# Graph attention: the decay and the division of a visit's sums moved from VectorE to GpSimd, between its gathers

## Chip, cores and metric

One Trainium2 chip, of which the kernel uses one core. The metric is the device time of one execution in microseconds (us), the median of several runs. The engines are TensorE (PE; its weight loads are PEld), VectorE (DVE), ScalarE (ACT), GpSimd (POOL) and SyncE (SP), which issues most transfers.

## What is computed

Four graph layers follow one another on 1250 nodes, 21250 edges and 1024 features, each with a residual sum and a layer norm behind it: a product with a sparse weight, graph attention, a graph convolution, and two neighbour-mean layers. The change lies in the attention:

```python
xl = (x @ Wl).reshape(n, H, D)
xr = (x @ Wr).reshape(n, H, D)
msg = xl[src] + xr[dst]
act = jnp.where(msg > 0, msg, NEG_SLOPE * msg)
e = jnp.einsum('ehd,hd->eh', act, att)
m = jax.ops.segment_max(e, dst, num_segments=n)
p = jnp.exp(e - m[dst])
denom = jax.ops.segment_sum(p, dst, num_segments=n)
alpha = p / (denom[dst] + 1e-16)
out = jax.ops.segment_sum(alpha[..., None] * xl[src], dst, num_segments=n)
```

with 4 heads of 64 columns.

## The kernel before

The attention is one loop over 23 visits (SUBS). A visit takes 55 nodes (SUB) and a window of 1024 edges, which are sorted by their target; the window has two halves (QUADS, index a), each of 4 tiles of 128 edges. A visit's work is spread over several visits' time, and each engine has its own program, written out by hand; semaphores alone tie them together. The main step i counts quarters of a visit, four to a visit.

- **GpSimd** gathers the rows xl[src]: for each half four indirect transfers of 128 rows (gather_half, L507, issued at L509). It has seven buffers (GOT), so the gather for a half waits until VectorE has weighed the half seven before (L1286), and with each new visit for that visit's source indices (L1282). In time, GpSimd gathers the second half of visit J+1 and the first half of visit J+2 while the other engines are at visit J.
- **SP** loads per visit the source indices (L1201), the targets spread over all partitions (L1206), the targets as columns (L1209) and the rows of xr (L1217). After the loads of visit j it stores the mixed rows of visit j-5 (STORE_LAG; store, L1245 to L1248, which waits for out_ready); then come a fetch of a weight tile for the later layers in some visits (L1223, visits 4, 4, 5, 5, 6, 9, 12, 15, 18, 21), in visit 17 loads for the next stage (load_ahead, L1236), and then the loads of visit j+1, the source indices first.
- **TensorE** forms the messages (L1308, L1313: it turns the gathered rows and adds the target's row), scores them (L1320), spreads scores (L1330), subtracts the new maximum (take_shift, L1336), turns the shifted score rows (turn, L1344) and sums the weighed rows per node (mix, L1353).
- **ScalarE** scales messages (L1430), marks nodes (L1419, L1425), takes the exponentials of the scores (L1450) and of the fall of the maximum (keep_sums, L1441): the factors by which older sums decay.
- **VectorE** bends messages (L1492), finds maxima (L1500), marks edges (L1524), clamps scores (L1530), weighs the gathered rows with the exponentials (weigh, L1537, two instructions a visit), splits a weight tile in some visits (low, L1568) and closes a visit with finish (L1543): the decay of the node's old sums (L1549), the addition of TensorE's new sums (L1552), a guard of the denominators (L1555), their reciprocal (L1557) and the division, a multiplication into the mixed rows (L1561). finish of visit j-3 is the last work of the main visit j; the clamp of the next visit stands right behind it.

The old sums are not zero before the first visit: they hold each node's own loop edge. They lie in one tile for all visits (summed), so no visit waits for another's sums.

Of the kernel before, what the change touches and what calls it, by code (L numbers as in the profile page):

```python
# [18 lines left out]
ALU = mybir.AluOpType  # L19
# [5 lines left out]
FEAT, HID, HEADS = 1024, 256, 4  # L25
HEAD_DIM = HID // HEADS
# [7 lines left out]
SUB = 55  # L34
SUBS = -(-NODES // SUB)
# [471 lines left out]
def gather_half(nc, got, src, a, xl_d, landed):  # L507
    for t in range(QUAD):
        nc.gpsimd.indirect_dma_start(got[:, t, :], None, xl_d,  # L509
                                     bass.IndirectOffsetOnAxis(src[:, a * QUAD + t:a * QUAD + t + 1], 0))\  # L510
            .then_inc(landed, 16)
# [593 lines left out]
def attention_stage(nc, g, src_d, dst_d, xl_d, xr_d, best, summed, x1_d, mixed_d, fetched, first_src, first_got,  # L1105
# [12 lines left out]
    with nc.Fori(0, rounds) as again, ExitStack() as ctx:  # L1118
        m = Memory(nc, ctx, "attention")

        def slots(name, shape, dtype=F32, n=2):
            return [m.sb(f"{name}{s}", shape, dtype) for s in range(n)]
# [17 lines left out]
        keep = slots("keep", [SUB, HEADS])  # L1140
        hot = slots("hot", [P, SUB_TILES + 1, SUB])
        weighted = slots("weighted", [P, SUB_TILES, HEADS, HEAD_DIM + 1])
        inverse = m.sb("inverse", [SUB, HEADS])
        mixed = slots("mixed", [SUB, HID])
        nothing = m.sb("nothing", [ROWS - SUB * SUBS, HEAD_DIM])
        message_ps = [m.ps(f"message_ps{s}", [P, HALF]) for s in range(2)]
# [16 lines left out]
        fall_ready, shift_ready, shifted, shifted_out, turned, clamp_ready, exp_ready, keep_ready, hot_ready = (  # L1163
            m.sem(n) for n in
            "fall_ready shift_ready shifted shifted_out turned clamp_ready exp_ready keep_ready hot_ready".split())
        weighed, mixed_in, out_ready = (m.sem(n) for n in "weighed mixed_in out_ready".split())
        best_found, lowered, summed_up, guarded, inverted = (
            m.sem(n) for n in "best_found lowered summed_up guarded inverted".split())
# [4 lines left out]
        mixed_stored = m.sems("mixed_stored")  # L1173
        block = m.block(gpsimd_works=True)

        def held(j, a):
            return got[(j * QUADS + a) % GOT]
# [7 lines left out]
        def half_of(u):  # L1185
            return u % QUADS, u // QUADS

        def pair_of(u):
            a, k = half_of(u)
            return 2 * (a * KH + k), 2 * (a * KH + k) + 2  # L1190

        @block.sync
        def _(sp):
# [83 lines left out]
        @block.gpsimd  # L1277
        def _(pool):
            for j in range(SUBS):
                s = j % 3  # L1280
                if j >= 1:
                    pool.wait_ge(src_ready[s], 16 * (j // 3 + (1 if s else 0)))  # L1282
                for a in range(QUADS):
                    n = j * QUADS + a
                    if n >= GOT:
                        pool.wait_ge(weighed, n - GOT + 1)  # L1286
                    if n >= 1:
                        gather_half(nc, held(j, a), src[s], a, xl_d, got_ready[n % GOT])
            pool.wait_ge(next_src, 16)
            pool.wait_ge(weighed, (SUBS * QUADS - 1) // GOT * GOT + 1)  # L1290
            gather_half(nc, first_got, first_src, 0, xl_d, next_got)
            pool.wait_ge(next_got, 16 * QUAD)

        @block.tensor
        def _(pe):
# [28 lines left out]
            def spread(j, u):  # L1324
                i = j * UNITS + u
                if u == 0:
                    pe.wait_ge(rows_ready, j + 1)
                elif i >= 2:
                    pe.wait_ge(maxed, i - 1)
                nc.tensor.matmul(spread_ps[u % 2][:, :], picked(g, *pair_of(u)), score_rows[:, :],  # L1330
                                 start=True, stop=True).then_inc(spread_out, 1)
# [81 lines left out]
        def _(act):  # L1413
# [23 lines left out]
            def keep_sums(j):  # L1437
                b = j % 2
                by_part = keep[b][:, :].rearrange("p (k t) -> p t k", t=2)
                for part in range(2):  # L1440
                    last = nc.scalar.activation(by_part[:, part, :], fall[b][part * PART:part * PART + SUB, :], ACT.Exp)  # L1441
                last.then_inc(keep_ready, 1)
# [19 lines left out]
            for i in range(LAST + 2 * UNITS):  # L1462
                j, q = i // UNITS, i % UNITS
                if q == 0 and 2 <= j <= SUBS + 1:
                    exponentials(j - 2)
                if i < LAST:
                    scale(i)
                if q == 0 and 2 <= j <= SUBS + 1:
                    keep_sums(j - 2)
                if q == 0 and j in SPLIT_VISITS:  # L1470
                    high(SPLIT_VISITS.index(j))
                if q == 1 and 1 <= j <= SUBS:
                    take_rows(j - 1)
                if q == (1 if j == 0 else 2) and j + 1 < SUBS:
                    mark_far(j + 1)
                if q == (2 if j == 0 else 3) and j + 1 < SUBS:
                    find_nodes(j + 1)
                if i == LAST + 2:
                    act.wait_ge(ahead_turned, 1)
                    nc.scalar.activation(ahead_hi[:, :], message_ps[0][:, 0:HID], ACT.Copy).then_inc(ahead_high, 1)  # L1480
                if q == 3 and 1 <= j <= SUBS:
                    take_shifted(j - 1)
# [3 lines left out]
        def _(dve):  # L1486
# [56 lines left out]
            def finish(j):  # L1543
                b = j % 2
                whole = summed[0:SUB, j]
                if j == SUBS - 1:
                    dve.wait_ge(keep_ready, j + 1)
                dve.wait_ge(mixed_in, j + 1)
                nc.vector.tensor_tensor(whole, whole, keep[b][:, :].unsqueeze(2)  # L1549
                                        .to_broadcast([SUB, HEADS, HEAD_DIM + 1]), ALU.mult).then_inc(lowered, 1)  # L1550
                dve.wait_ge(lowered, j + 1)
                nc.vector.tensor_tensor(whole, mix_ps[b][0:SUB, 0:HEADS * (HEAD_DIM + 1)]  # L1552
                                        .rearrange("p (h d) -> p h d", h=HEADS), whole, ALU.add).then_inc(summed_up, 1)
                dve.wait_ge(summed_up, j + 1)
                nc.vector.tensor_scalar(inverse[:, :], whole[:, :, HEAD_DIM], 1e-16, None, ALU.add).then_inc(guarded, 1)  # L1555
                dve.wait_ge(guarded, j + 1)
                nc.vector.reciprocal(inverse[:, :], inverse[:, :]).then_inc(inverted, 1)  # L1557
                dve.wait_ge(inverted, j + 1)
                if j >= 2:
                    dve.wait_ge(mixed_stored[b], 16 * (j // 2))  # L1560
                nc.vector.tensor_tensor(mixed[b][:, :].rearrange("p (h d) -> p h d", h=HEADS), whole[:, :, 0:HEAD_DIM],  # L1561
                                        inverse[:, :].unsqueeze(2).to_broadcast([SUB, HEADS, HEAD_DIM]), ALU.mult)\
                    .then_inc(out_ready, 1)

            def low(n):
                k, columns = n // 2, slice(n % 2 * HALF, (n % 2 + 1) * HALF)
# [32 lines left out]
            for i in range(LAST + 3 * UNITS):  # L1599
                j, q = i // UNITS, i % UNITS  # L1600
# [758 lines left out]
```

## Time and profile before

| | us |
|---|---|
| median of 3 runs | 1559.93 |
| lowest and highest run | 1555.97, 1564.11 |
| span of the profiled execution, first to last instruction | 1553.5 |
| busy in it: TensorE | 1433.6 |
| VectorE | 783.6 |
| ScalarE | 421.9 |
| GpSimd | 254.4 |

The profiled execution is known by its span; the runs' times lie 2.5 to 10.6 us above it. The attention runs from about 310 to 650 us of the span; ahead of it the graph is built and the first layer computed, behind it come the other layers, in which TensorE works almost without a break. A row of the timeline has the start, the duration, the engine, the line of the kernel, the operation, what it writes and reads, and in brackets how long the engine was idle before it and what ended that. "issue" means that the profile shows nothing for which it waited; SPq is SP's queue, where a row is the issue of a transfer.

### The profile page before, as it was taken

How to read it: one execution, taken by the hardware profiler on the slowest of the kernel's cores; microseconds unless marked ns; L12 is line 12 of the kernel's file. 1: busy time of each engine (PE TensorE's matmuls, PEld its weight loads, DVE VectorE, ACT ScalarE, POOL GpSimd, SP SyncE). 2: the span in 40 equal slices, each digit the busy share in tenths (PEclk: the TensorE clock that was granted, in tenths of full speed). 3: DMA queues.
4: the chain of work that ended last, by engine and by line, in shares of the span. 5: the costliest groups of instructions: out<-in, count | busy, mean ns of one | idle time of the engine just before them, and what ended most of it. 6: DMA issues, size and time to landing. Idle time of an engine off the chain costs nothing.

```text
span 1553.5 us, 17781 instructions
## 1 busy us (share of the span) xinstructions
PE 1433.6 (92%) x6845; PEld 1145.2 (74%) x6845; DVE 783.6 (50%) x1359; ACT 421.9 (27%) x716; POOL 254.4 (16%) x309
## 2 busy tenths in 40 slices
PE   3988999748999989899999999999999999999996
PEld 3876888625666656678888888888888888888884
DVE  6996776517888868754336632221033232411243
ACT  7853222235565545312111100110120001201000
POOL 3000000064666655110000010000000100000000
PEclk9997999969999999999999999999999999999998
DMA  1665344454555644152117552230056544400252
GB/s 46 192 181 189 106 126 116 93 157 150 163 155 153 179 146 130 55 185 85 61 42 240 180 189 85 103 145 1 0 190 219 187 124 147 143 1 0 91 194 95
DMA packets 101988, 195.95 MB, mean 126 GB/s; under 512 B 26856, under 2 KB 61465, under 8 KB 101905
## 3 DMA queue, kind: packets, MB, share of 16 engines
q1 hardware_dynamic: 77434, 121.01, 25.8%
q0 software_dynamic: 22800, 73.61, 13.9%
q8 instruction: 54, 0.88, 0.2%
q10 hardware_dynamic: 1670, 0.21, 0.1%
q14 instruction: 30, 0.24, 0.0%
HBM read 140.86 MB, written 53.92 MB: 125 GB/s over the span
## 4 chain that ended last, share of the span: by engine, by line
PE 56%; DVE 1%; DMA 0%; issue 0%; POOL 0%; DVEq 0%; ACT 0%
PE layers_y_ps L1927 35%; PE layers_y_ps L1948 17%; PE layers_turn_ps L1911 2%; PE layers_up_ps L1894 1%; PE layers_y_ps L1964 1%; DMA x_d<-fetched_x 0%; DVE layers_w_lo L2082 0%; DVE layers_y L2126 0%; PE layers_y_ps L1972 0%; DVE layers_y L597 0%; DVE layers_ln_stats L591 0%; PE layers_turn_ps L1882 0%; DVE layers_parts_lo L2099 0%; DVEq L592 0%; PE layers_y_ps L1882 0%
## 5 line engine op out<-in xcount | busy, mean ns | idle before, releaser
L1948 PE MATMUL layers_y_ps<-layers_parts_hi,layers_counts 128*128 128x512 f32 x464 | 143.6, 391 | 0.0
L1948 PE MATMUL layers_y_ps<-layers_parts_lo,layers_counts 128*128 128x512 f32 x464 | 143.3, 390 | 0.0
L1927 PE MATMUL layers_y_ps<-layers_w_hi,layers_parts_hi 128*128 128x512 f32 x400 | 126.0, 396 | 0.0
L1927 PE MATMUL layers_y_ps<-layers_w_lo,layers_parts_hi 128*128 128x512 f32 x400 | 123.6, 390 | 0.0
L1927 PE MATMUL layers_y_ps<-layers_w_hi,layers_parts_lo 128*128 128x512 f32 x400 | 123.5, 390 | 0.0
L509 POOL DMA_INDIRECT attention_got<-xl_d,attention_src x104 | 106.5, 1024 | 63.1 <-DVE attention_weighted L1537 31.3
L1948 PEld LDWEIGHTS layers_y_ps<-layers_parts_lo,layers_counts 128*128 128x128 f32 x464 | 87.1, 188 | 18.7
L1948 PEld LDWEIGHTS layers_y_ps<-layers_parts_hi,layers_counts 128*128 128x128 f32 x464 | 86.9, 188 | 18.9
L1353 PE MATMUL attention_mix_ps<-attention_weighted,attention_hot 128*110 128x260 f32 x368 | 95.7, 384 | 3.7 <-DVE attention_weighted L1537 3.7
L1320 PE MATMUL attention_row_ps<-attention_bent,edges_att_rows 128*128 128x512 f32 x184 | 97.1, 611 | 0.0
L2099 DVE SCALAR_TENSOR_TENSOR layers_parts_lo<-layers_y_ps,layers_parts_hi 128x1024 fp32r<-128x1024 f32 x16 | 19.6, 1225 | 147.5 <-ACT layers_parts_hi L2043 147.5
L2093 DVE TENSOR_TENSOR layers_parts_lo<-layers_turn_ps,layers_parts_hi 128x1024 fp32r<-128x1024 f32 x24 | 29.4, 1224 | 125.8 <-ACT layers_parts_hi L2037 125.8
L2037 ACT ACTIVATE layers_parts_hi<-layers_turn_ps 128x1024 fp32r<-128x1024 f32 x24 | 24.6, 1026 | 246.6 <-PE layers_turn_ps L1911 246.6
L1353 PEld LDWEIGHTS attention_mix_ps<-attention_weighted,attention_hot 128*110 128x110 f32 x368 | 61.9, 175 | 38.5 <-DVE attention_weighted L1537 14.9
L1927 PEld LDWEIGHTS layers_y_ps<-layers_w_lo,layers_parts_hi 128*128 128x128 f32 x400 | 75.1, 188 | 16.4
L1927 PEld LDWEIGHTS layers_y_ps<-layers_w_hi,layers_parts_lo 128*128 128x128 f32 x400 | 75.1, 188 | 16.1
L1927 PEld LDWEIGHTS layers_y_ps<-layers_w_hi,layers_parts_hi 128*128 128x128 f32 x400 | 73.3, 188 | 14.4
L1927 PE MATMUL layers_y_ps<-fetched_w_hi,layers_parts_hi 128*128 128x512 f32 x240 | 76.0, 398 | 0.0
L1927 PE MATMUL layers_y_ps<-fetched_w_lo,layers_parts_hi 128*128 128x512 f32 x240 | 75.5, 395 | 0.0
L1927 PE MATMUL layers_y_ps<-fetched_w_hi,layers_parts_lo 128*128 128x512 f32 x240 | 75.4, 395 | 0.0
L1492 DVE TENSOR_TENSOR attention_bent<-attention_message_ps,attention_scaled 128x512 f32<-128x512 f32 x92 | 61.8, 685 | 22.8 <-issue 11.8
L1430 ACT ACTIVATE attention_scaled<-attention_message_ps 128x512 f32<-128x512 f32 x92 | 54.4, 591 | 68.2 <-PE attention_message_ps L1313 45.3
(341 smaller groups left out, 2783.4 us busy)
## 6 DMA issues: line engine op xcount, KB each, us to landing
layers_counts<-counts_d SPq DMA_DIRECT2D x30, 640.0 KB, 4.0
layers_rest<-x_d SPq DMA_DIRECT2D x23, 512.0 KB, 4.1
self_d<-layers_y POOLq DMA_DIRECT2D x20, 512.0 KB, 6.0
x_d<-layers_y POOLq DMA_DIRECT2D x19, 512.0 KB, 2.9
fetched_x<-x_d SPq DMA_DIRECT2D x17, 512.0 KB, 3.7
fetched_raw<-in_L_gnn_W_self POOLq DMA_DIRECT2D x16, 512.0 KB, 5.9
fetched_raw<-in_L_gnn_W_neigh POOLq DMA_DIRECT2D x16, 512.0 KB, 9.0
heads_dst_wide<-in_dst_held SPq DMA_DIRECT2D x13, 512.0 KB, 4.0
```

The lines of the kernel that those rows point to most:

```text
L509: nc.gpsimd.indirect_dma_start(got[:, t, :], None, xl_d, bass.IndirectOffsetOnAxis(src[:, a * QUAD + t:a * QUAD + t + 1], 0))\
L1320: nc.tensor.matmul(row_ps[j % 2][:, :], g["att_rows"][:, k, (1 - a) * HEADS:(1 - a) * HEADS + P], bent[i % 3][:, :], start=(i % UNITS == 0 ...
L1353: last = nc.tensor.matmul(mix_ps[j % 2][0:2 * SUB, 0:HEADS * (HEAD_DIM + 1)], hot[j % 2][:, t:t + 2, :].rearrange("p t n -> p (t n)"), wei ...
L1430: nc.scalar.activation(scaled[i % 2][:, :], message_ps[i % 2][:, :], ACT.Copy, scale=SLOPE)\
L1492: nc.vector.tensor_tensor(bent[i % 3][:, :], message_ps[i % 2][:, :], scaled[i % 2][:, :], ALU.max)\
L1894: last = nc.tensor.matmul(up_ps[:, a:a + HALF], rows_in[t % 2][:, k, :], w[k][:, a:a + HALF], start=(k == 0 and p == 0), stop=(k == KH - 1 ...
L1911: last = nc.tensor.transpose(turn_ps[:, k * P:(k + 1) * P], rows_in[:, k * P:(k + 1) * P], g["ident"][:, :])
L1927: last = nc.tensor.matmul(y_ps[n % 2][:, a:a + HALF], rows_in[t][:, k * P:(k + 1) * P], w[k][:, a:a + HALF], start=(k == 0 and p == 0), st ...
L1948: last = nc.tensor.matmul(y_ps[n % 2][:, a:a + HALF], counts[c % 2][:, k, :], part[k][:, a:a + HALF], start=(k == 0 and part is hi), stop= ...
L2037: nc.scalar.activation(hi[t], turn_ps[:, :], ACT.Copy).then_inc(turned_high, 1)
L2093: nc.vector.tensor_tensor(lo[t], turn_ps[:, :], hi[t].bitcast(F32), ALU.subtract).then_inc(turned_low, 1)
L2099: nc.vector.scalar_tensor_tensor(out=lo[t], in0=y_ps[n % 2][:, :], scalar=scale, in1=hi[t].bitcast(F32), op0=ALU.mult, op1=ALU.subtract).t ...
```

## The change

The decay (now lower) and the division (now divide) of every visit but the last go to GpSimd. In GpSimd's visit j the decay of visit j-4 stands between the two blocks of gathers, and the division of visit j-5 behind the second block; the rest follows the last gathers. The reciprocals get a second buffer. ScalarE's keep factors wait until those of two visits before have been used, since they have two buffers. For the last visit VectorE does both itself.

```diff
-        inverse = m.sb("inverse", [SUB, HEADS])
+        inverse = slots("inverse", [SUB, HEADS])
...
+        def lower(engine, queue, j):
+            whole = summed[0:SUB, j]
+            queue.wait_ge(keep_ready, j + 1)
+            engine.tensor_tensor(whole, whole, keep[j % 2][:, :].unsqueeze(2)
+                                 .to_broadcast([SUB, HEADS, HEAD_DIM + 1]), ALU.mult).then_inc(lowered, 1)
+
+        def divide(engine, queue, j):
+            b = j % 2
+            queue.wait_ge(inverted, j + 1)
+            if j >= 2:
+                queue.wait_ge(mixed_stored[b], 16 * (j // 2))
+            engine.tensor_tensor(mixed[b][:, :].rearrange("p (h d) -> p h d", h=HEADS), summed[0:SUB, j, :, 0:HEAD_DIM],
+                                 inverse[b][:, :].unsqueeze(2).to_broadcast([SUB, HEADS, HEAD_DIM]), ALU.mult)\
+                .then_inc(out_ready, 1)
...
                     if n >= 1:
                         gather_half(nc, held(j, a), src[s], a, xl_d, got_ready[n % GOT])
+                    if a == 0 and j >= 4:
+                        lower(nc.gpsimd, pool, j - 4)
+                    if a == 1 and j >= 5:
+                        divide(nc.gpsimd, pool, j - 5)
+            for j in range(SUBS - 5, SUBS - 1):
+                if j > SUBS - 5:
+                    lower(nc.gpsimd, pool, j)
+                divide(nc.gpsimd, pool, j)
             pool.wait_ge(next_src, 16)
...
             def keep_sums(j):
+                if j >= 2:
+                    act.wait_ge(lowered, j - 1)
...
             def finish(j):
                 if j == SUBS - 1:
-                    dve.wait_ge(keep_ready, j + 1)
+                    dve.wait_ge(lowered, j)
+                    lower(nc.vector, dve, j)
                 dve.wait_ge(mixed_in, j + 1)
-                nc.vector.tensor_tensor(whole, whole, keep[b][:, :].unsqueeze(2)
-                                        .to_broadcast([SUB, HEADS, HEAD_DIM + 1]), ALU.mult).then_inc(lowered, 1)
                 dve.wait_ge(lowered, j + 1)
...
-                nc.vector.tensor_scalar(inverse[:, :], whole[:, :, HEAD_DIM], 1e-16, None, ALU.add).then_inc(guarded, 1)
+                if 2 <= j:
+                    dve.wait_ge(out_ready, j - 1)
+                nc.vector.tensor_scalar(inverse[b][:, :], whole[:, :, HEAD_DIM], 1e-16, None, ALU.add).then_inc(guarded, 1)
                 dve.wait_ge(guarded, j + 1)
-                nc.vector.reciprocal(inverse[:, :], inverse[:, :]).then_inc(inverted, 1)
-                dve.wait_ge(inverted, j + 1)
-                if j >= 2:
-                    dve.wait_ge(mixed_stored[b], 16 * (j // 2))
-                nc.vector.tensor_tensor(mixed[b][:, :].rearrange("p (h d) -> p h d", h=HEADS), whole[:, :, 0:HEAD_DIM],
-                                        inverse[:, :].unsqueeze(2).to_broadcast([SUB, HEADS, HEAD_DIM]), ALU.mult)\
-                    .then_inc(out_ready, 1)
+                nc.vector.reciprocal(inverse[b][:, :], inverse[b][:, :]).then_inc(inverted, 1)
+                if j == SUBS - 1:
+                    dve.wait_ge(out_ready, j)
+                    divide(nc.vector, dve, j)
```

GpSimd's queue in the attention, from the second half of visit 3 to the first half of visit 7, as the difference of the two orders (the numbers behind names are buffers; x4 is a block of four gathers):

```order
 L509 DMA heads_first_got<-xl_d,heads_first_src 128x256 x4
 L509 DMA attention_got0<-xl_d,attention_src0 128x256 x4
+L1195 TENSOR_TENSOR heads_summed<-heads_summed,attention_keep0 55x260
 L509 DMA attention_got1<-xl_d,attention_src0 128x256 x4
 L509 DMA attention_got2<-xl_d,attention_src1 128x256 x4
+L1195 TENSOR_TENSOR heads_summed<-heads_summed,attention_keep1 55x260
 L509 DMA attention_got3<-xl_d,attention_src1 128x256 x4
+L1203 TENSOR_TENSOR attention_mixed0<-heads_summed,attention_inverse0 55x256
 L509 DMA attention_got4<-xl_d,heads_first_src 128x256 x4
```

The decay (L1195 of the changed kernel) comes between the two blocks of a visit, the division (L1203) between a visit's second block and the next visit's first, which reads new source indices.

VectorE's queue at the end of a main visit with a weight split, up to the next visit's weighing, before:

```order
L1519 COPY heads_best<-attention_new_best1 128x2
L1568 TENSOR_TENSOR fetched_w_lo0<-fetched_raw2,fetched_w_hi0 128x512
L1549 TENSOR_TENSOR heads_summed<-heads_summed,attention_keep1 55x260
L1552 TENSOR_TENSOR heads_summed<-attention_mix_ps1,heads_summed 55x260
L1555 TENSOR_SCALAR attention_inverse<-heads_summed 55x4
L1557 RECIPROCAL attention_inverse<-attention_inverse 55x4
L1561 TENSOR_TENSOR attention_mixed1<-heads_summed,attention_inverse 55x256
L1530 TENSOR_SCALAR attention_clamped<-attention_row_ps1 128x32
L1537 TENSOR_TENSOR attention_weighted1<-attention_got0,attention_weighted1 128x16x64
```

and with the change, at the same place:

```order
L1544 COPY heads_best<-attention_new_best1 128x2
L1591 TENSOR_TENSOR fetched_w_lo0<-fetched_raw2,fetched_w_hi0 128x512
L1576 TENSOR_TENSOR heads_summed<-attention_mix_ps1,heads_summed 55x260
L1581 TENSOR_SCALAR attention_inverse1<-heads_summed 55x4
L1583 RECIPROCAL attention_inverse1<-attention_inverse1 55x4
L1555 TENSOR_SCALAR attention_clamped<-attention_row_ps1 128x32
L1562 TENSOR_TENSOR attention_weighted1<-attention_got0,attention_weighted1 128x16x64
```

Two instructions are gone from it, the decay ahead of the addition and the division behind the reciprocal.

SP's queue, whose order stays as it was, shown from the changed kernel, from a visit's rows of xr to the next visit's source indices:

```order
L1232 DMA attention_xr2<-xr_hi_d 64x256
L1232 DMA attention_xr2<-xr_lo_d 64x256
L1262 DMA mixed_d<-attention_mixed1 55x256
L1210 TENSOR_LOAD edges_edge_first
L1210 ISA x2
L1216 ISA
L1216 DMA heads_first_src<-in_src_held 128x8
```

The store (L1262, before L1247) stands ahead of the next source indices (L1216, before L1201), and it waits for the division, which GpSimd now does.

## Rows read from the trace of the kernel before

**Rows 1.** Stretches: us, busy of PE, PEld, DVE, ACT, POOL, then PEclk, DMA share, GB/s.
```profile
434.00:546.00 112.00, 105.21 (x479) 69.65 (x478) 94.38 (x226) 66.52 (x105) 72.56 (x70) 1.00 0.57 169
```

**Rows 2.** Timeline of VectorE around the end of a visit.
```profile
457.99 0.41 DVE L1549 TENSOR_TENSOR heads_summed<-heads_summed,attention_keep 55x260 f32<-55x260 f32 x1
...
459.30 0.42 DVE L1561 TENSOR_TENSOR attention_mixed<-heads_summed,attention_inverse 55x256 f32<-55x256 f32 x1
460.17 0.19 DVE L1530 TENSOR_SCALAR attention_clamped<-attention_row_ps 128x32 f32<-128x32 f32 x1 [0.46 <-PE attention_row_ps L1344]
460.69 2.36 DVE L1537 TENSOR_TENSOR attention_weighted<-attention_got,attention_weighted 128x1024 f32<-128x1024 f32 x2 [0.32 <-issue]
```

**Rows 3.** Waits from 300 to 655 us: engine, line, releaser, total us, times, longest.
```profile
PE attention_message_ps L1308 <- DVE attention_bent L1492: 11.2, 17, 0.7
...
PE attention_mix_ps L1353 <- DVE attention_weighted L1537: 3.7, 6, 1.1
```

**Rows 4.** Timeline of VectorE, the clamp of one later visit.
```profile
547.76 0.17 DVE L1530 TENSOR_SCALAR attention_clamped<-attention_row_ps 128x32 f32<-128x32 f32 x1
```

**Rows 5.** Timeline of GpSimd over two visits.
```profile
462.18 1.68 POOL L509 DMA_INDIRECT attention_got<-xl_d,attention_src  x1 [2.04 <-DVE attention_weighted L1537]
...
467.92 0.95 POOL L509 DMA_INDIRECT attention_got<-xl_d,heads_first_src  x1 [0.31 <-issue]
...
471.67 0.94 POOL L509 DMA_INDIRECT attention_got<-xl_d,heads_first_src  x1 [0.30 <-issue]
475.35 1.68 POOL L509 DMA_INDIRECT attention_got<-xl_d,heads_first_src  x1 [2.74 <-DVE attention_weighted L1537]
```

**Rows 6.** Timeline of SP: plain visit, visit with a fetch, visit 17.
```profile
459.74 0.35 SPq L1247 DMA_DIRECT2D mixed_d<-attention_mixed  x1
461.57 0.09 SPq L1201 DMA_DIRECT2D heads_first_src<-in_src_held  x1
...
471.63 0.35 SPq L1247 DMA_DIRECT2D mixed_d<-attention_mixed  x1
...
473.99 0.01 SPq L1201 DMA_DIRECT2D attention_src<-in_src_held  x1
...
536.01 0.35 SPq L1247 DMA_DIRECT2D mixed_d<-attention_mixed  x1
...
540.45 0.35 SPq L1201 DMA_DIRECT2D heads_first_src<-in_src_held  x1
```

**Rows 7.** Landing of one index tile's loads; GpSimd's next gather after the last of rows 6.
```profile
DMA to landing us min/median/max: 0.8/1.3/1.8
...
545.41 0.94 POOL L509 DMA_INDIRECT attention_got<-xl_d,heads_first_src  x1 [1.56 <-DMA heads_first_src<-in_src_held]
```

**Rows 8.** Timelines: ends of GpSimd's blocks, and readers on TensorE.
```profile
390.38 0.94 POOL L509 DMA_INDIRECT attention_got<-xl_d,attention_src  x1 [0.30 <-issue]
...
613.12 0.95 POOL L509 DMA_INDIRECT attention_got<-xl_d,attention_src  x1 [0.30 <-issue]
...
621.90 0.60 PE L1308 MATMUL attention_message_ps<-all_ident,attention_got 128*128 128x128 f32 x4
...
327.31 0.95 POOL L509 DMA_INDIRECT attention_got<-xl_d,attention_src  x1 [0.30 <-issue]
...
331.80 0.63 PE L1308 MATMUL attention_message_ps<-all_ident,attention_got 128*128 128x128 f32 x4 [1.62 <-DMA attention_got<-xl_d,attention_src]
```

**Rows 9.** Groups of GpSimd: line, operation, shape, count, then busy us and mean ns.
```profile
L160 POOL IOTA setup_iota_i<- 128x1280 int32 x1 | 1.2, 1215 | 0.0
...
L158 POOL TENSOR_SCALAR_AFFINE_SELECT all_ident<-all_ident 128x128 f32<-128x128 f32 x1 | 0.3, 292 | 0.2 <-POOL all_ident L156 0.2
```

**Rows 10.** Timelines at the end of the attention.
```profile
636.08 1.34 POOL L509 DMA_INDIRECT heads_first_got<-xl_d,heads_first_src  x1 [0.30 <-issue]
...
642.48 0.17 DVE L1557 RECIPROCAL attention_inverse<-attention_inverse 55x4 f32<-55x4 f32 x1
...
651.46 0.66 PE L1882 MATMUL layers_y_ps<-all_ident,fetched_mixed 128*128 128x128 f32 x2 [6.21 <-PEq L99]
```

## The prediction

> **What bounds the kernel now.** I read the busy time by stretches first. In the middle of the attention TensorE is busy 105.2 of 112 us, VectorE 94.4 and GpSimd 72.6 [rows 1]: TensorE sets the pace, VectorE has little air, GpSimd a third of its time. Next came the timeline of VectorE at the end of a visit, to see what the moved work is worth there. The decay takes 0.41 us and the division 0.42 us, and between them stay the addition, the guard and the reciprocal; but the clamp of the next visit, which stands right behind, starts only 0.45 us after the division ends, because it waits for TensorE's turn of the score rows [rows 2]. So VectorE's chain before the clamp is mostly not what ends last. What TensorE waits for VectorE is all after the clamp: 11.2 us in 17 waits for a bent message and 3.7 us in 6 waits for weighed rows [rows 3]. That sum, 14.9 us, bounds what faster VectorE work could give.
>
> Then I read the two queues that the work moves to or past. GpSimd gathers eight times 128 rows in each visit, in two blocks of four, one for each half of a visit's edges. A block takes 4.69 us when nothing holds it (467.92 to 472.61). The second-half block waits for VectorE's weighing, idle 2.04 us ahead of 462.18 and 2.74 us ahead of 475.35 [rows 5]. That idle time is GpSimd's whole reserve. On SP the store of a visit's mixed rows stands **ahead** of the next load of source indices, in order: store at 459.74, just after VectorE's division ended at 459.72, and source indices at 461.57, so 1.83 us later [rows 6, 2]. Those indices are what GpSimd's next first-half block needs; it begins at 467.92, long after they landed [rows 5].
>
> **The change part by part.** *VectorE* loses two instructions a visit, 0.83 us and two hand-overs. I count it at nothing: it comes out of the stretch ahead of a clamp that already waits 0.46 us [rows 2], and below something else becomes later. If that cover were gone, the gain is bounded by the 14.9 us above.
>
> *ACT's new wait* (the keep factors two visits back must have been used) and *VectorE's new waits* (the decay done; the division two visits back done, for the second inverse buffer) concern GpSimd work that is over a visit or more earlier; I count nothing. Behind ACT's wait stand its scalings, for which VectorE waits; if the cover went, each visit would lose the lateness of one multiplication.
>
> *GpSimd* gains 19 decays and 18 divisions up to its last visit, and 7 multiplications in the tail. No row shows a multiplication on GpSimd. Lower bound: VectorE's 0.41 us. Upper bound: the iota of 1280 columns, 1.22 us. Between them: iota 1280 columns in 1.22 us, select 128 columns in 0.29 us [rows 9], so 0.80 ns a column and 0.19 us fixed; two inputs of 260 columns, 520 read, give 0.61 us. I take 0.61, since GpSimd's own rows are nearer than VectorE's. The Trainium skill ("GPSIMD Engine Reference", section 3.1) speaks against the move: a two-input addition of 2048 columns took 1.96 times as long on GpSimd as on VectorE. As an estimate by that ratio a multiplication here is 0.81 us and the sum below 6.8 us higher; no run here shows it yet.
>
> *The order of the queues is the main term.* In GpSimd's visit j the division of visit j-5 stands behind the second-half block, and SP's store of visit j-5 waits for it. Behind that store, on the same queue, is the load of the source indices for j+1, for which GpSimd's very next block, the first half of j+1, waits. Before, VectorE released that store at the end of its own visit, at 459.72; now the division can begin only where the next block began, at 467.92, some 8 us later [rows 2, 5]. So a closed chain arises: second-half gathers, division, store, index load, first-half gathers, decay, and again second-half gathers. Its length, from rows:
> - two blocks of gathers, 2 x 4.69 = 9.38 us [rows 5];
> - from store to index load on SP, 1.83 us [rows 6];
> - landing of the indices, 1.3 us, the median (0.8 to 1.8) [rows 7];
> - decay and division, 2 x 0.61 = 1.22 us;
> - a gap of 0.30 us, as between gathers [rows 5], at each of the two multiplications, 0.60 us.
>
> That is **14.33 us a visit**. The reserve of 2.0 to 2.7 us is not enough: 17 such chains lie between the block that ends at 391.32 (before the first division) and the last block, which ended at 614.07 [rows 8]. Before they took 222.75 us, 13.1 each. Now 17 x 14.33 = 243.6 us, 20.9 more. On top, all on SP between store and index load: eight fetches of a weight tile, each 473.99 - 471.63 - 1.83 = 0.53 us, 4.2 in sum; and in visit 17 the loads ahead, 540.45 - 536.01 - 1.83 = 2.6 us [rows 6], whose indices then came 4.96 us after issue instead of 1.3 (545.41 [rows 7]), 3.7 more. Together 31.4 us. From it goes the lead that gathers have at the end: the last block ended at 614.07 and its first reader ran at 621.90; landing takes 3.5 us (328.26 to 331.80, where TensorE did wait) [rows 8], so 4.3 us of lead are used up first. **Sum: 31.4 - 4.3 = 27.1 us.** From about the eighth visit on, TensorE then waits for gathered rows in the middle of each visit.
>
> *The tail:* GpSimd's last four gathers, which ended at 637.42, now stand behind the division that follows the reciprocal at 642.65 [rows 10]: 642.65 + 0.3 + 0.61 + 4.69 = 648.3, and 3.5 us to land make 651.8, against TensorE's restart at 651.46 with a barrier ahead of it [rows 10]. I add 1 us. The layers behind the attention shift as a whole.
>
> Against the profiled execution the sum is 1553.5 + 28 = 1581.5 us of span. The median of the runs is 1559.93, 6.4 above the span, so **1588 us**.
>
> Ends of the unknowns: multiplications at 0.42, landing 0.8, one gap of 0.3 instead of two and no slow landing in visit 17 make a chain of 13.15 us, so 223.6 + 4.2 + 2.6 - 222.75 - 4.3 = +3.3 us. Multiplications at 1.22 and landing 1.8 make 16.05 us, +56 us, and 2 for the tail. My own case lies between 1563 and 1618.
>
> **The rivals.**
> *Faster.* The chain is hidden, because GpSimd's divisions come early enough or indices land at once, and VectorE's 0.83 us shorten each visit. For it: one visit, where the clamp found TensorE's turn done, started it at 547.76, right behind the division [rows 4]; there each tenth saved ahead would have come through. It decides once GpSimd's chain is shorter than the 13.1 us that a visit took on average. Against it: 9.38 us of gathers and 1.83 us on SP are already 11.2 before any multiplication or landing. Price at most 14.9 us: 1545. Chance 0.08.
> *No change.* The chain is about as long as a visit now, 13.1 us: multiplications as on VectorE, landing 0.8. 1560 to 1567. Chance 0.09.
> *Slower still: the two engines get in each other's way.* The first gather behind the weighing takes 1.68 us instead of 0.95, 0.73 more; it starts at 462.18, while VectorE multiplies two SBUF tiles until about 463.05 [rows 5, 2]. If each of the 34 multiplications in the chains were late by that, 34 x 0.73 = 25 us come on top: 1613. Against it: gathers that lie beside VectorE's other work keep 0.95. The Trainium skill ("SBUF — State Buffer", Who interferes with whom) states that a VectorE instruction with two SBUF inputs and a GpSimd instruction that reads SBUF shut each other out for a whole instruction; the long first gather agrees with that, but it does not prove it. Chance 0.13.
> My own case keeps 0.70. That the change moves nothing is excluded: the order of the program shows both multiplications between the gathers.
>
> **How the numbers follow.** A measurement of this kernel can tell about 0.5% (7.8 us) from no change. Slower by more than that are my case and the last rival, 0.83; within it 0.09; faster 0.08. The range takes in no change on one side and the worst sum on the other: 1556 to 1620, which leaves out the faster rival and some 0.1 above. In the likeliest case alone it is 1563 to 1618.
>
> **What would show it.** Right: GpSimd's second-half block no longer waits for VectorE's weighing, but its first-half block for the load of source indices, 3 to 4 us a visit; SP's store waits for GpSimd; index loads start about 8 us later within a visit; TensorE waits for gathered rows about 1.5 us a visit from visit 8 or so on; last gather near 645 instead of 614. Multiplications on GpSimd at 0.5 to 0.8 us confirm the price. Wrong: GpSimd still idle for the weighing in each visit (the chain is hidden), or TensorE's new idle time behind VectorE or ACT instead (then a wait that I count at nothing is what costs).

## The result and the profile after

The changed kernel takes **1611.84 us** (median; 1609.22 to 1613.35), the kernel before, run beside it, 1557.95 us (1553.69 to 1564.11): ratio 1.0347, 95% interval 1.0313 to 1.0380, some 54 us slower. Slower was forecast, by the mechanism that the traces then showed, but 1588 us. Four executions at a far lower granted clock (0.65 to 0.80, 2094 to 2679 us) are in the medians of the table further down but not in its ratios; without them these medians are 1560.11 us (decay alone), 1555.25 (store later, next gathers first), 1600.86 (weighing with a PSUM input) and 1552.87 (before, in the last row).

The profiled execution of the changed kernel spans 1607.2 us, 53.7 more than before (1553.5). The same stretch as in [rows 1], in the same columns:

```profile
434.00:546.00 112.00, 90.42 (x378) 59.22 (x378) 70.91 (x167) 53.11 (x83) 69.83 (x71) 0.94 0.42 122
```

TensorE falls from 105.2 to 90.4 us busy, and VectorE and ScalarE with it; TensorE's granted clock (PEclk) is 0.94 there instead of 1.00. GpSimd is at 69.8 of 112 us, so the busy shares name no engine that has become the bound. The waits do; columns as in [rows 3], here over the whole span. First the queue of SP, then GpSimd, TensorE and ScalarE:

```profile
SPq L1262 <- POOL attention_mixed L1203: 151.3, 14, 13.6
...
POOL attention_got L509 <- DMA attention_src<-in_src_held: 42.0, 10, 6.1
...
POOL attention_got L509 <- DMA heads_first_src<-in_src_held: 25.8, 5, 7.2
...
POOL heads_first_got L509 <- DMA attention_src<-in_src_held: 7.9, 2, 4.5
...
POOL heads_first_got L509 <- DMA heads_first_src<-in_src_held: 3.5, 1, 3.5
...
PE attention_row_ps L1367 <- ACT attention_shifted_rows L1471: 34.9, 13, 6.0
...
PE attention_message_ps L1331 <- DMA attention_got<-xl_d,attention_src: 6.2, 6, 1.3
...
PE attention_message_ps L1331 <- DMA attention_got<-xl_d,heads_first_src: 3.9, 5, 1.6
...
ACT attention_far L1442 <- DMA heads_dst_wide<-in_dst_held: 32.7, 8, 7.3
ACT attention_far L1442 <- DMA attention_dst_wide<-in_dst_held: 24.8, 8, 4.6
```

SP's store (L1262) waits 151 us for GpSimd's division, GpSimd's gathers wait 79.2 us in 18 waits for the load of source indices that stands behind that store (3.0 of it before the first store), and TensorE waits. One round of it, GpSimd first, then SP:

```profile
533.69 1.92 POOL L509 DMA_INDIRECT attention_got<-xl_d,attention_src  x1 [0.30 <-issue]
535.62 0.78 POOL L1203 TENSOR_TENSOR attention_mixed<-heads_summed,attention_inverse 55x256 f32<-55x256 f32 x1
539.75 0.98 POOL L509 DMA_INDIRECT attention_got<-xl_d,heads_first_src  x1 [3.35 <-DMA heads_first_src<-in_src_held]
...
544.50 0.63 POOL L1195 TENSOR_TENSOR heads_summed<-heads_summed,attention_keep 55x260 f32<-55x260 f32 x1
545.29 0.98 POOL L509 DMA_INDIRECT attention_got<-xl_d,heads_first_src  x1 [0.16 <-issue]
...
550.50 0.78 POOL L1203 TENSOR_TENSOR attention_mixed<-heads_summed,attention_inverse 55x256 f32<-55x256 f32 x1
556.21 0.98 POOL L509 DMA_INDIRECT attention_got<-xl_d,attention_src  x1 [4.94 <-DMA attention_src<-in_src_held]
```
```profile
536.42 0.35 SPq L1262 DMA_DIRECT2D mixed_d<-attention_mixed  x1
537.96 0.36 SPq L1216 DMA_DIRECT2D heads_first_src<-in_src_held  x1
...
551.30 0.35 SPq L1262 DMA_DIRECT2D mixed_d<-attention_mixed  x1
551.70 0.36 SPq L1238 DMA_DIRECT2D fetched_raw<-in_L_gnn_W  x1
553.01 0.34 SPq L1216 DMA_DIRECT2D attention_src<-in_src_held  x1
```

The division ends at 536.40, the store goes out at 536.42, the index load at 537.96, the next gather starts at 539.75: each waits for the one ahead, and GpSimd idles 3.35 us. In the next round a fetch lies between store and index load, and it idles 4.94 us. In [rows 5] GpSimd's first-half blocks began without a wait.

The multiplications themselves, all 22 of each on GpSimd (ns min/median/max, first and last start), with VectorE's one of each:

```profile
L1195 POOL TENSOR_TENSOR heads_summed<-heads_summed,attention_keep x22: 609/631/896, 369.2 to 684.3; 55x260 f32<-55x260 f32 x22
L1195 DVE TENSOR_TENSOR heads_summed<-heads_summed,attention_keep x1: 396/396/396, 690.9 to 690.9; 55x260 f32<-55x260 f32 x1
...
L1203 POOL TENSOR_TENSOR attention_mixed<-heads_summed,attention_inverse x22: 602/628/777, 389.4 to 688.2; 55x256 f32<-55x256 f32 x22
L1203 DVE TENSOR_TENSOR attention_mixed<-heads_summed,attention_inverse x1: 418/418/418, 692.3 to 692.3; 55x256 f32<-55x256 f32 x1
```

They cost 0.63 us, near the estimate of 0.61. The estimate's price of a column came from two other operations, and no run varies the width, so the agreement bears out the sum and not that price. The Trainium skill ("GPSIMD Engine Reference", section 3.1) had 1.96 times VectorE's time, for 2048 columns; here it is 0.63 against 0.40 to 0.42, about 1.5.

**Where the 53.7 us come from.** The last block of gathers and its reader on TensorE:

```profile
663.66 0.94 POOL L509 DMA_INDIRECT attention_got<-xl_d,attention_src  x1 [0.30 <-issue]
```
```profile
667.84 0.60 PE L1331 MATMUL attention_message_ps<-all_ident,attention_got 128*128 128x128 f32 x4
```

The 17 chains, from the block that ends at 389.37 to the one that ends at 664.60, take 275.2 us instead of 222.7 [rows 8]: +52.5. They begin 2.0 us earlier (389.37 instead of 391.32), and the lead of the last block over its reader falls from 7.8 to 3.2 us: -4.6. From that reader to the end of the span it was 1553.5 - 621.9 = 931.6 us and is 1607.2 - 667.8 = 939.4: +7.8, the tail. Together 52.5 - 2.0 - 4.6 + 7.8 = 53.7.

### The profile page after: what moved, and what is told of

Read it like the earlier page. It is cut to its first block, busy times and chain, and to the rows that moved or that the text cites. A ratio compares the mean times of both kernels' runs of the same rounds, so it can differ in the third digit from the quotient of the medians.

```text
span 1607.2 us, 17825 instructions
## 1 busy us (share of the span) xinstructions
PE 1448.8 (90%) x6845; PEld 1153.9 (72%) x6845; DVE 769.4 (48%) x1315; ACT 422.6 (26%) x716; POOL 284.1 (18%) x353
## 4 chain that ended last, share of the span: by engine, by line
PE 54%; DVE 1%; DMA 0%; issue 0%; POOL 0%; DVEq 0%; ACT 0%
PE layers_y_ps L1950 33%; PE layers_y_ps L1971 17%; PE layers_turn_ps L1934 2%; PE layers_up_ps L1917 1%; PE layers_y_ps L1987 1%; DMA x_d<-fetched_x 0%; DVE layers_w_lo L2105 0%; DVE layers_y L2149 0%; PE layers_y_ps L1995 0%; DVE layers_y L597 0%; DVE layers_ln_stats L591 0%; PE layers_turn_ps L1905 0%; DVE layers_parts_lo L2122 0%; DVEq L592 0%; PE layers_y_ps L1905 0%
## 5 line engine op out<-in xcount | busy, mean ns | idle before, releaser
L1343 PE MATMUL attention_row_ps<-attention_bent,edges_att_rows 128*128 128x512 f32 x184 | 102.4, 641 | 0.0
L2122 DVE SCALAR_TENSOR_TENSOR layers_parts_lo<-layers_y_ps,layers_parts_hi 128x1024 fp32r<-128x1024 f32 x16 | 19.6, 1225 | 147.3 <-ACT layers_parts_hi L2066 147.3
L2116 DVE TENSOR_TENSOR layers_parts_lo<-layers_turn_ps,layers_parts_hi 128x1024 fp32r<-128x1024 f32 x24 | 29.4, 1224 | 125.4 <-ACT layers_parts_hi L2060 125.4
```

The lines of the kernel that those rows point to most:

```text
L1343: nc.tensor.matmul(row_ps[j % 2][:, :], g["att_rows"][:, k, (1 - a) * HEADS:(1 - a) * HEADS + P], bent[i % 3][:, :], start=(i % UNITS == 0 ...
L2116: nc.vector.tensor_tensor(lo[t], turn_ps[:, :], hi[t].bitcast(F32), ALU.subtract).then_inc(turned_low, 1)
L2122: nc.vector.scalar_tensor_tensor(out=lo[t], in0=y_ps[n % 2][:, :], scalar=scale, in1=hi[t].bitcast(F32), op0=ALU.mult, op1=ALU.subtract).t ...
```

## The experiments

Theory: the chain is closed because the store that waits for GpSimd stands ahead of the index load that GpSimd waits for; the multiplications cost nothing where they are off that chain. Rivals: they cost by themselves, or through VectorE; or ScalarE's wait for the wide load is what lengthens a visit. In the table "chains" is the stretch of 17 visits and "tail" the stretch to the end, both taken from each trace as above.

| kernel | median us | before us | ratio (95% interval) | chains us | tail us |
|---|---|---|---|---|---|
| before (profiled) | | | | 222.7 | 931.6 |
| the change | 1611.84 | 1557.95 | 1.0347 (1.0313 to 1.0380) | 275.2 | 939.4 |
| decay alone | 1562.50 | 1553.89 | 1.0045 (1.0024 to 1.0067) | 224.2 | 931.2 |
| division alone | 1599.68 | 1553.89 | 1.0286 (1.0255 to 1.0316) | 262.0 | 940.7 |
| store a visit later | 1560.24 | 1553.89 | 1.0034 (1.0017 to 1.0050) | 219.1 | 939.2 |
| division mid-visit | 1566.38 | 1553.89 | 1.0085 (1.0058 to 1.0111) | 223.9 | 939.8 |
| store later, next gathers first | 1555.51 | 1553.55 | 1.0005 (0.9989 to 1.0021) | 219.3 | 932.6 |
| index load ahead of the store | 1561.68 | 1553.55 | 1.0064 (1.0044 to 1.0085) | 220.0 | 938.8 |
| weighing with a PSUM input | 1602.10 | 1553.55 | 1.0306 (1.0271 to 1.0341) | 264.6 | 938.8 |
| fetch ahead of the store | 1601.39 | 1553.55 | 1.0311 (1.0282 to 1.0339) | 265.5 | 939.0 |
| index load alone behind | 1606.76 | 1553.27 | 1.0341 (1.0310 to 1.0371) | 269.7 | 939.2 |

**The decay alone on GpSimd.**

```diff
-                    if a == 1 and j >= 5:
-                        divide(nc.gpsimd, pool, j - 5)
...
-                if j == SUBS - 1:
-                    dve.wait_ge(out_ready, j)
-                    divide(nc.vector, dve, j)
+                divide(nc.vector, dve, j)
```

> Only the decay is left on GpSimd; the division is VectorE's again, so VectorE releases the store. Closed-chain theory (division, store, index load behind it on SP, gathers, decay, gathers): the chain is open, GpSimd needs 2 x 4.74 of gathers and 0.65 for the decay, some 11 of 13.1 us a visit, and the index loads come early again: 1552 to 1563 us, no difference from before. Rival (GpSimd's multiplications and VectorE's get in each other's way, each by its share): about half of the 54 us stays, 1575 to 1595.

Measured 1562.50 us: the chains are back at 224.2 us and GpSimd waits for the weighing again. The theory holds, the rival falls. What stays, 0.45%, lies at the edge of what can be told, and its cause was not looked for.

**The division alone.**

```diff
-                    if a == 0 and j >= 4:
-                        lower(nc.gpsimd, pool, j - 4)
...
                 dve.wait_ge(mixed_in, j + 1)
+                lower(nc.vector, dve, j)
```

> Only the division is left on GpSimd, the decay is VectorE's again. Closed-chain theory: the chain stands as it was, less the decay and its gap, 17 x (0.65 + 0.16) = 14 us less than the change: 1594 to 1602 us. Rival (each multiplication costs its share wherever the store hangs): about half, 1575 to 1590.

Measured 1599.68 us, as the theory has it, but the 13.2 us by which the chains shorten (14 expected) are not all the decay. Between the two blocks of a visit the 17 chains spend 5.1 us instead of 14.0, 8.8 less: the decay goes, and the gap of 0.30 us between gathers comes back. Another 4.7 us come from shorter second-half blocks, 87.9 instead of 92.6 us in sum, which the sum in the expectation did not have; that it nearly met 14 is in part luck.

**The store one visit later.**

```diff
-    STORE_LAG, AHEAD_VISIT, AHEAD_NEEDS = 5, 17, -(-len(fetched.mixed) * P // SUB)
+    STORE_LAG, AHEAD_VISIT, AHEAD_NEEDS = 6, 17, -(-len(fetched.mixed) * P // SUB)
```

> The whole change, with each store one visit later on SP, so that it is ready when SP comes to it and the index load behind it isn't held. Closed-chain theory: of the 54 us only the 8 us in the tail stay: 1556 to 1570 us; GpSimd's first-half block no longer waits for the load of source indices, and its second-half block waits for the weighing as before. Rival (GpSimd's multiplications, or gathers lengthened beside VectorE's weighing, cost by themselves): 1590 or more.

Measured 1560.24 us. One number takes away nearly all of the loss, with every multiplication still on GpSimd. Its waits:

```profile
POOL attention_got L509 <- DVE attention_weighted L1562: 22.4, 11, 2.8
...
POOL attention_got L509 <- DMA attention_src<-in_src_held: 3.0, 1, 3.0
...
SPq L1262 <- POOL attention_mixed L1203: 26.7, 4, 11.3
...
PE attention_row_ps L1367 <- ACT attention_shifted_rows L1471: 0.9, 2, 0.7
```

GpSimd's waits for indices fall from 79.2 us (42.0 + 25.8 + 7.9 + 3.5) to 3.0, and it waits for the weighing again, as in [rows 5]. What is left is the tail.

**The division right behind the decay.**

```diff
-                    if a == 1 and j >= 5:
+                    if a == 0 and j >= 5:
                         divide(nc.gpsimd, pool, j - 5)
```

> The whole change, with the division right behind the decay, ahead of the second-half block instead of behind it. The index load then goes out about 1.8 us after the division, while GpSimd gathers the second half for 4.7 to 5.4 us, so store, issue and landing (1.8 + 2.7 = 4.5 us) are covered. Closed-chain theory: a visit of GpSimd is 4.74 + 5.45 + 2 x 0.7 = 11.6 us, below the 13.1 us of a visit: 1556 to 1570 us, the tail's 8 us included. Rival (multiplications cost by themselves): 1605 or more.

Measured 1566.38 us. The store still waits for GpSimd (89.6 us in 17 waits), but store, issue and landing now lie beside the second-half block: the chains take 223.9 us. It is not the wait that costs but what it closes. Of the 0.85% that stays, the tail is 8.2 us; the rest was not looked for.

**The tail: the next round's gathers ahead of the last two divisions** (with the store one visit later).

```diff
+                if j == SUBS - 3:
+                    pool.wait_ge(next_src, 16)
+                    pool.wait_ge(weighed, (SUBS * QUADS - 1) // GOT * GOT + 1)
+                    gather_half(nc, first_got, first_src, 0, xl_d, next_got)
                 divide(nc.gpsimd, pool, j)
...
-            gather_half(nc, first_got, first_src, 0, xl_d, next_got)
```

> The kernel with the store one visit later, and in the tail the four gathers for the next round ahead of the last two divisions instead of behind them. If the tail's 8 us come from those gathers standing behind the divisions, the stretch from TensorE's last second half to the end goes back from 939.2 to about 931.6 us, and the time to 1548 to 1555 us, 2 to 4 us below before (VectorE's freed time). Rival (the tail is late because of the divisions' stores or the layers' own start): it stays at 939, 1558 to 1563 us.

Measured 1555.51 us, ratio 1.0005: a little above the range, and no difference from before. The tail went as expected, 939.2 to 932.6 us. The trace says why it was late: at the end of the attention GpSimd drains. Instructions of L1118 in the kernel before (ns, start us):

```profile
L1118 POOLq DRAIN  x1: 7563/7563/7563, 639.4 to 639.4; - x1
```

In the changed kernel, and in this one:

```profile
L1118 POOLq DRAIN  x1: 7563/7563/7563, 695.7 to 695.7; - x1
```
```profile
L1118 POOLq DRAIN  x1: 8082/8082/8082, 643.2 to 643.2; - x1
```

Before, it ran from 639.4 to 647.0, beside VectorE's last work, ahead of TensorE's restart at 651.46 [rows 10]. In the change GpSimd's last gathers end at 693.8, the drain runs from 695.7 to 703.3, and TensorE restarts only at 704.92, 13.7 us after its last matmul:

```profile
704.92 0.66 PE L1905 MATMUL layers_y_ps<-all_ident,fetched_mixed 128*128 128x128 f32 x2 [13.75 <-PEq L99]
```

With the gathers first the drain ends at 651.3, and TensorE restarts here:

```profile
652.94 0.66 PE L1906 MATMUL layers_y_ps<-all_ident,fetched_mixed 128*128 128x128 f32 x2 [6.83 <-PEq L99]
```

In the change and here alike that is 1.7 us after the drain's end. Before, the drain was over 4.5 us ahead of the restart, so there it was not what ended last. The chains are 3.4 us shorter than before (219.3 against 222.7), near the 2 to 4 us expected of VectorE's freed time, but the time is not; that VectorE's time is what shortens them was not tested by itself.

**The index load ahead of the store, the wide load behind it.**

```diff
                         .then_inc(src_ready[j % 3], 16)
+                if j >= STORE_LAG + 1:
+                    store(j - STORE_LAG - 1)
                 if j >= 2:
                     sp.wait_ge(far_ready, j - 1)
```

> The whole change, and on SP the load of source indices goes ahead of the store that waits for GpSimd's division; the wide load of destinations, for which ScalarE's marking of far edges waits, stays behind it. Theory (the chain closes through the index load alone): 1556 to 1572 us, the tail's 8 us included, although ScalarE still waits for the wide load. Rival (ScalarE's wait of 3 to 5 us a visit costs by itself): 1580 to 1610 us.

Measured 1561.68 us, chains 220.0: the index load alone opens the chain. ScalarE's wait for the wide load shrinks to one of 2.0 us, since the store is now late in three visits only (26.1 us from 390 to 612 us), so this run does not price that wait. The next does.

**The counterpart: wide load ahead of the store, index load behind it.**

```diff
+                if j >= 1:
+                    sp.dma_start(wide[j % 2][:, :], dst_d[window].partition_broadcast(P)).then_inc(wide_ready[j % 2], 16)
+                if j >= STORE_LAG + 1:
+                    store(j - STORE_LAG - 1)
...
                 if j >= 1:
                     sp.dma_start(src[j % 3][:, :], src_d[window].rearrange("(p t) -> p t", p=P))\
```

> The counterpart of the kernel with the index load ahead of the store: here the wide load of destinations goes ahead of the store, and the index load alone (with what follows it) stays behind. Theory (the chain closes through the index load): GpSimd's chain is as long as with the whole change, 1600 to 1613 us; ScalarE's waits for the wide load (57 us in sum) are gone, and TensorE now waits for gathered rows instead of ScalarE's shifted rows. Rival (ScalarE's wait for the wide load is what lengthens a visit, or half of it): 1560 to 1590 us.

Measured 1606.76 us, ratio 1.0341, against 1.0347 for the change. ScalarE no longer waits for the wide load at all, and nothing is gained. TensorE's waits:

```profile
PE attention_message_ps L1331 <- DMA attention_got<-xl_d,attention_src: 22.9, 12, 3.3
...
PE attention_message_ps L1331 <- DMA attention_got<-xl_d,heads_first_src: 13.2, 6, 3.8
...
PE attention_message_ps L1331 <- DMA heads_first_got<-xl_d,attention_src: 6.4, 3, 2.8
```

42.5 us for gathered rows, against 10.1 in the change, took the place of the 34.9 for ScalarE's shifted rows, of which 0.7 are left. ScalarE was the messenger: its load hung from the same store.

**Why the second-half block is long: the weighing with its second input in PSUM.**

```diff
-                                        weighted[b][:, tiles, :, HEAD_DIM:].rearrange("p t h d -> p (t h) d")
+                                        row_ps[b][:, SPARE:SPARE + QUAD * HEADS].unsqueeze(2)
                                         .to_broadcast([P, QUAD * HEADS, HEAD_DIM]), ALU.mult)\
```

> The whole change, but VectorE's weighing takes its second input from PSUM instead of SBUF (other numbers of the same count, so the weighed values are not those of the reference). Theory (the second-half block is longer because gathers lie beside a VectorE instruction with two SBUF inputs): the block goes from 5.45 to about 4.75 us, 17 x 0.7 = 12 us less, 1597 to 1604 us. Rival (the gathers are held by something else, other transfers or their own queue): the block keeps 5.3 to 5.5 us, and the time 1608 to 1615 us.

Measured 1602.10 us; the second-half block falls from 5.45 to 4.88 us on average (17 blocks), the chains by 10.6 us. In the change, VectorE's weighing and the gathers beside it:

```profile
548.44 2.36 DVE L1562 TENSOR_TENSOR attention_weighted<-attention_got,attention_weighted 128x1024 f32<-128x1024 f32 x2 [0.33 <-ACT attention_weighted L1475]
```
```profile
547.83 0.94 POOL L509 DMA_INDIRECT attention_got<-xl_d,heads_first_src  x1 [0.30 <-issue]
549.08 1.41 POOL L509 DMA_INDIRECT attention_got<-xl_d,heads_first_src  x1 [0.30 <-issue]
```

In this kernel:

```profile
543.53 2.35 DVE L1563 TENSOR_TENSOR attention_weighted<-attention_got,attention_row_ps 128x1024 f32<-128x1024 f32 x2 [0.33 <-issue]
```
```profile
543.53 0.94 POOL L509 DMA_INDIRECT attention_got<-xl_d,heads_first_src  x1 [0.30 <-issue]
544.77 0.94 POOL L509 DMA_INDIRECT attention_got<-xl_d,heads_first_src  x1 [0.30 <-issue]
```

The weighing lasts as long (2.35 us), yet in no round of this kernel does a gather that starts beside it take more than 0.98 us. With two SBUF inputs they took up to 1.96, as the first row of the round shown for the change does (1.92). Nine gathers of 1.1 to 1.5 us remain in the attention, and the trace says why. One of them, with what VectorE does beside it:

```profile
541.97 1.25 POOL L509 DMA_INDIRECT attention_got<-xl_d,heads_first_src  x1 [0.30 <-issue]
```
```profile
541.71 0.69 DVE L1592 TENSOR_TENSOR fetched_w_lo<-fetched_raw,fetched_w_hi 128x512 fp32r<-128x512 f32 x1
```

All nine start beside the weight split (L1592) or the marking of edges (L1550), two other instructions of VectorE that take both inputs from SBUF, and each ends 0.8 to 0.9 us after that instruction.

**Why the landing is long: the fetch ahead of the store.**

```diff
-                if j >= STORE_LAG:
-                    store(j - STORE_LAG)
                 for k, visit in enumerate(FETCH_VISITS):
                     if j == visit:
                         fetch(k)
+                if j >= STORE_LAG:
+                    store(j - STORE_LAG)
```

> The whole change, with the fetch of a weight tile ahead of the store on SP instead of between store and index load. Theory (the index load lands 1.8 us after issue when nothing is ahead of it and about 3 or more behind a fetch of 512 KB, seven visits, 11.5 us in sum, and 1.6 us of issue): landing falls to 1.8 us in these visits and the time to 1596 to 1602 us. Rival (landing is slow for another reason, such as the gathers still under way): 1608 to 1614 us.

Measured 1601.39 us. The 17 times from index load to first gather, summed, fall from 45.4 to 36.5 us, those from the division's end to the index load from 30.8 to 29.4. The round that had the fetch in the change, now without it on SP between store and load, and the gather that followed:

```profile
546.76 0.35 SPq L1262 DMA_DIRECT2D mixed_d<-attention_mixed  x1
548.32 0.36 SPq L1216 DMA_DIRECT2D attention_src<-in_src_held  x1
```
```profile
550.12 0.98 POOL L509 DMA_INDIRECT attention_got<-xl_d,attention_src  x1 [3.38 <-DMA attention_src<-in_src_held]
```

From load to gather it is 1.80 us instead of 3.20 (553.01 to 556.21). Three of the 17 stay at 3 us or more without a fetch; one is visit 17 with its loads ahead, the other two stay open.

## Why the prediction was right in kind and too small

**The closed chain** was right, link by link, and so were its place (store ahead of index load on SP), the price of a multiplication, the use of the lead (4.3 predicted, 4.6 measured) and the cover of ScalarE's and VectorE's added waits (the changed kernel's trace shows no wait of either for GpSimd's multiplications). The runs that reorder the store, the index load and the wide load on SP show it, one order each.

**The sizes.** Predicted for the 17 chains 243.6 + 4.2 + 2.6 + 3.7 = 254.1 us, measured 275.2. By terms, in sums over the 17 (predicted, measured):

| term | predicted | measured |
|---|---|---|
| index load to first gather | 25.8 | 45.4 |
| second-half block | 79.7 | 92.6 |
| first-half block | 79.7 | 80.6 |
| division's end to index load, fetches included | 37.9 | 30.8 |
| two multiplications | 20.7 | 22.6 |
| gaps at them | 10.2 | 3.3 |

- *"Landing of the indices, 1.3 us, the median"* failed most, +19.6 us. The 1.3 us of [rows 7] is from the issue to the landing; from the issue to the first gather, with neither a fetch nor the loads ahead in between, it is 1.8 to 2.1 us in eight of nine visits. And a fetch between store and load was priced by the time that its issue takes on SP (0.53 us), not by its transfer; behind one fetch the first gather starts 1.0 to 2.6 us later than that, and 3.0 behind two. Moving the fetch alone shortened the chains by 9.7 us.
- *"Two blocks of gathers, 2 x 4.69"* failed next, +12.9 for the second-half blocks. The block of 4.69 us was one without a weighing beside it. Both second-half blocks of [rows 5] begin with a gather of 1.68 us beside the weighing, and over the same 17 visits of the kernel before, the second-half block took 5.39 us on average. The number was in the trace, and the rival about engines in each other's way had the mechanism: I applied it to the multiplications, where it costs 0.15 us at times (0.78 instead of 0.63), and not to the gathers. That its 1613 us is near the measured time is chance: it had 25 us there, and the PSUM run gives 10.6.
- *"The tail: I add 1 us"* was +7.8. The block of gathers took 4.8 us (4.69 counted); the sum put only a landing of 3.5 us behind it, and there the drain of 7.56 us stands, which is in the trace of before but hidden there, and was not looked up.
- SP's interval and the gaps were too high, together by 14 us, which hid a part of the rest.

That the measured time lies within the range is in part luck: its upper end came from multiplications at 1.22 us and a landing of 1.8 us, and the multiplications, worth 21 us of it, took 0.63 us.

**VectorE's 0.83 us** were counted at nothing. With the chain open the 17 visits gain 2.7 to 3.6 us (219.1 to 220.0 against 222.7), 0.2 us a visit, and with the tail mended the time is that of before. That fits the cover named (a clamp that waits for TensorE), which no run tests by itself. No version here is faster than the kernel before.

**Where TensorE would wait** was wrong: mostly at the turn, for ScalarE, and little for gathered rows. Two loads hang from the late store, and the one that ScalarE needs was overlooked. By the prediction's own sign this idle time behind ScalarE would have spoken against the sum, as a wait counted at nothing; the two runs that put one of these loads ahead of the store show that it hangs from the same store and adds nothing to the chain.

## What to carry to other kernels

Before a step is moved to another engine, follow who waits for its result on an in-order queue and what stands behind that wait: here a store, and behind it the load that the new engine needs next. The remedy is in the queue's order, by one place or one visit, not in the step. Take the length of a link from all its rows under the load that it will have, not from a clean one, and count a transfer's time, not only its issue; and look at what an engine does at the end of a stage after its last instruction.

## What the runs showed of the hardware

- **GpSimd's drain** at the end of the stage took 7.56 us in three of the four traces where it was read and 8.08 in the fourth. In the same places ScalarE's took 0.32 to 0.33 us and VectorE's 0.02. TensorE restarted 1.6 to 1.7 us after GpSimd's drain where that came last.
- **Gathers and VectorE.** A gather that starts while VectorE multiplies two SBUF tiles lasts as if held until that instruction ends: beside a weighing of two instructions of 1.2 us that began at 533.57, the gather from 533.69 took 1.92 us, which is to the end of the first instruction and 0.9 more. With the second input in PSUM it is 0.94 to 0.98, and the nine longer ones left end 0.8 to 0.9 us after another VectorE instruction with two SBUF inputs. The Trainium skill ("SBUF — State Buffer", Who interferes with whom) says that an instruction of VectorE with two SBUF inputs contends with one of GpSimd that reads SBUF; the PSUM run agrees, with gathers as that instruction of GpSimd.
- **A small load behind a large one.** In the changed kernel the reader of 4 KB of indices starts 1.8 to 2.1 us after their issue in eight of nine visits (3.3 in the ninth), 2.8 to 4.4 us when a 512 KB load was issued 1.3 us earlier on the same queue, and 4.8 behind two of them.
